# One scan step for two states of one channel block, in a fused AdaLN / Mamba / recurrent kernel

## The chip, the cores and the metric

The kernel runs on one core of one Trainium2 chip. The metric is device time in microseconds (us) of one execution; lower is better. The kernel before took 1357.22 us in the median of three runs (1354.40, 1357.22 and 1361.41).

## What is computed

Two layers run over x of shape (4, 1024, 256). Each layer is adaptive layer norm, a mixer with a gated residual, layer norm, a second part with a gated residual. Layer 0 has dilated attention and a linear layer on block-quantised values. Layer 1 has a Mamba block (a state space scan) and a recurrent gate network. The change is in the scan. Cut to that, the reference is:

```python
xb = silu(causal_conv(x_branch))                    # (B, T, 512 channels)
x_ssm = xb @ x_proj_w                               # B_t, C_t: 16 states each; dt: 1
dt = softplus(dt @ dt_proj_w + dt_proj_b)
A_bar = exp(dt[..., None] * A)                      # (B, T, 512, 16)
Bx = dt[..., None] * B_t[:, :, None, :] * xb[..., None]
def step(h, inp):                                   # over T = 1024, for 512 x 16 states
    a, bx, c = inp
    h = a * h + bx
    return h, jnp.einsum('bds,bs->bd', h, c)
y = (ys + D_param * xb) * silu(z)
out = y @ c_proj_w
```

## The kernel before, in words

The work is cut into G = 8 **halves**: 4 batch rows, each in two halves of TH = 512 time steps. Halves 0, 2, 4, 6 start a batch row, and halves 1, 3, 5, 7 go on from the last states of the half before ("even" and "odd" halves below). The 512 channels are KD = 4 **channel blocks** of 128 partitions. Each block has 16 states, so a half has 64 scans of 512 time steps. They are done in STEPS = 32 **steps** of two scans, 256 steps in all; step m of half g is 32 g + m.

In the kernel before, a step takes one state s of two channel blocks, 2p and 2p+1. These are its operations:

- SyncE fetches row s of B_t and of C_t, broadcast over the 128 partitions (`sp_scan`, 256 KB each, three buffers each).
- ScalarE writes the decay exp(dt A) of each scan into a PSUM bank (`act_decay`, L1200). Scan n uses bank n % 3 and is done in place (`state_bank`, L280). Two of each half's decays, numbers 61 and 62 (`AHEAD`), are computed ahead into SBUF (K[3]) instead, before the softplus of the next half takes ScalarE.
- GpSimd writes dt B_t x for both blocks, 128x1024 (`pool_scan`, L1856), into one of three `inp` buffers once the scans of three steps ago have read it.
- VectorE does the two scans (L1638), copies their last column in even halves (L1646, `carried`), multiplies the states by C_t into one of three `hc` buffers (L1652) and at a block's end multiplies the sum by silu(z) (`dve_gate`, L1611). Where a step's two states lie in banks 2 and 0, copy and product are each done in two instructions (`state_pairs`, L292).
- TensorE adds the two products to two PSUM banks, Y and Y+1, one for each block (`pe_scan`, L846, an identity matmul), which ScalarE has opened with D x (L1227, semaphore dx).

While the scan of half g runs, the same engines do everything else for its neighbours: attention, linear layer, convolution, x_proj and softplus of half g+1 (`*_before`), and c_proj (L780), z (`pe_z`, L677, one PSUM bank, so each waits until VectorE has read the one before, z_ev, L1510), the gate network (L685, L693) and its sums for half g-1 (`*_after`). Each engine's order is written by `in_time` (L127): generators with due times from the table `TIMES`, in quarters of a step, are merged with the engine's scan part. Nothing is reordered later, so an instruction that waits holds all that is queued behind it on its engine.

## Time and profile before

| what | value |
|---|---|
| median of 3 runs | 1357.22 us |
| the profiled execution's own time | 1349.22 us |
| its span, first to last instruction | 1347.9 us |
| VectorE busy | 1243.0 us (92%) |
| TensorE busy | 1156.6 us (86%) |
| GpSimd busy | 984.0 us (73%) |
| ScalarE busy | 808.6 us (60%) |
| DMA traffic | 179.67 MB, 133 GB/s |
| granted TensorE clock, mean | 0.962 |

PE is the matmul part of TensorE and PEld its weight load, DVE is VectorE, ACT ScalarE, POOL GpSimd, SP SyncE. Busy time is the union of an engine's instructions; successive instructions on DVE and ACT overlap in the records by some 80 ns, so the sum of durations is above the busy time. A matmul of float32 shows as two records. "Idle before" is the time in which the engine had nothing running just before the instruction, and the name behind the arrow is what ended it.

### The profile page before, as it was taken

How to read it: one execution, taken by the hardware profiler on the slowest of the kernel's cores; microseconds unless marked ns; L12 is line 12 of the kernel's file. 1: busy time of each engine (PE TensorE's matmuls, PEld its weight loads, DVE VectorE, ACT ScalarE, POOL GpSimd, SP SyncE). 2: the span in 40 equal slices, each digit the busy share in tenths (PEclk: the TensorE clock that was granted, in tenths of full speed). 3: DMA queues.
4: the chain of work that ended last, by engine and by line, in shares of the span. 5: the costliest groups of instructions: out<-in, count | busy, mean ns of one | idle time of the engine just before them, and what ended most of it. 6: DMA issues, size and time to landing. Idle time of an engine off the chain costs nothing.

```text
span 1347.9 us, 12755 instructions
## 1 busy us (share of the span) xinstructions
PE 1156.6 (86%) x3576; PEld 635.3 (47%) x3576; DVE 1243.0 (92%) x1720; ACT 808.6 (60%) x1348; POOL 984.0 (73%) x521
## 2 busy tenths in 40 slices
PE   7667867798999989998999989998999989589984
PEld 5524432473446543574347543564347443333543
DVE  4668999999999999999999999999999999999986
ACT  3247454765777665865776665865776565645432
POOL 3206885689768986899769986899759986885832
PEclk9888988899999999999999999999999999899997
DMA  7304335432534344342534354343533343474611
GB/s 258 117 7 137 109 112 174 115 121 83 181 116 133 112 151 155 127 147 96 177 119 134 109 154 155 123 142 109 167 118 129 110 158 105 131 252 139 220 55 78
DMA packets 92023, 179.67 MB, mean 133 GB/s; under 512 B 10400, under 2 KB 15648, under 8 KB 91696
## 3 DMA queue, kind: packets, MB, share of 16 engines
q1 hardware_dynamic: 88928, 169.55, 39.1%
q10 hardware_dynamic: 3024, 9.31, 1.9%
q8 instruction: 28, 0.46, 0.1%
q14 instruction: 43, 0.35, 0.1%
HBM read 167.51 MB, written 11.31 MB: 133 GB/s over the span
## 4 chain that ended last, share of the span: by engine, by line
DVE 50%; PE 19%; issue 14%; ACT 12%; POOL 4%; DMA 0%; DVEq 0%; SPq 0%; POOLq 0%; ACTq 0%
DVE ps L1638 25%; DVE arena L1652 10%; DVE ps L1346 4%; PE ps L846 4%; PE ps L550 3%; ACT ps L1200 2%; ACT arena L870 2%; POOL arena L1856 2%; DVE stats_before L1239 2%; ACT arena L861 1%; PE ps L596 1%; PE ps L558 1%; PE ps L780 1%; PE ps L677 1%; DVE arena L1611 1%
## 5 line engine op out<-in xcount | busy, mean ns | idle before, releaser
L1856 POOL TENSOR_TENSOR arena<-arena 128x1024 f32<-128x1024 f32 x255 | 598.6, 2363 | 173.1 <-DVE ps L1638 144.6
L1638 DVE TENSOR_TENSOR_SCAN ps<-ps,arena 128x512 f32<-128x512 f32 x498 | 603.6, 1247 | 29.5 <-ACT ps L1200 18.4
L846 PE MATMUL ps<-arena,identF 128*128 128x512 f32 x1024 | 482.0, 603 | 35.8 <-DVE arena L1652 33.6
L1200 ACT ACTIVATE ps<-arena,negA 128x512 f32<-128x512 f32 x498 | 323.8, 683 | 232.0 <-DVE arena L1652 231.0
L1652 DVE TENSOR_TENSOR arena<-ps,arena 128x1024 f32<-128x1024 f32 (+1 forms) x341 | 317.1, 951 | 3.4 <-PE ps L846 0.9
L846 PEld LDWEIGHTS ps<-arena,identF 128*128 128x128 f32 x1024 | 191.5, 194 | 258.5 <-issue 186.3
L861 ACT ACTIVATE arena<-arena,rnln 128x256 f32<-128x256 f32 x128 | 66.2, 589 | 42.8 <-POOL rnln L1668 42.1
L1666 POOL TENSOR_TENSOR rnln<-vnln,consts 128x4 f32<-128x4 f32 x32 | 33.3, 1042 | 74.7 <-DVE vnln L1255 74.7
L596 PE MATMUL ps<-arena,inw 128*128 128x512 f32 x128 | 65.8, 663 | 19.5 <-ACT arena L870 13.3
L677 PE MATMUL ps<-arena,inw 128*128 128x512 f32 x128 | 65.3, 635 | 19.1 <-DVE arena L1510 19.1
L1346 DVE SCALAR_TENSOR_TENSOR ps<-arena,vecs,ps 128x512 f32<-128x512 f32 x96 | 64.7, 749 | 6.6 <-ACT ps L973 6.5
L438 PE MATMUL ps<-identF,arena 128*128 128x128 f32 x248 | 38.6, 299 | 34.5 <-ACT arena L861 17.8
L870 ACT ACTIVATE arena<-ps,modT 128x512 f32<-128x512 f32 x45 | 54.0, 1267 | 16.5 <-PE ps L438 15.8
L780 PE MATMUL ps<-cpw,arena 128*128 128x256 f32 x224 | 57.1, 410 | 6.3 <-DVE arena L1611 6.1
L780 PEld LDWEIGHTS ps<-cpw,arena 128*128 128x128 f32 x224 | 54.6, 327 | 10.6 <-DVE arena L1611 7.3
L438 PEld LDWEIGHTS ps<-identF,arena 128*128 128x128 f32 x248 | 29.9, 153 | 60.8 <-ACT arena L861 18.1
L1677 POOL TENSOR_TENSOR arena<-arena 128x512 f32<-128x512 f32 x42 | 52.9, 1271 | 6.3 <-ACT arena L1042 3.2
L1790 POOL TENSOR_TENSOR arena<-arena 128x1024 f32<-128x1024 f32 x14 | 32.9, 2352 | 33.0 <-ACT arena L1082 33.0
L596 PEld LDWEIGHTS ps<-arena,inw 128*128 128x128 f32 x128 | 25.2, 209 | 58.8 <-issue 26.9
L550 PE MATMUL ps<-arena,wqT 128*128 128x128 f32 (+2 forms) x128 | 40.8, 469 | 10.1 <-ACT arena L870 10.1
L677 PEld LDWEIGHTS ps<-arena,inw 128*128 128x128 f32 x128 | 24.3, 196 | 51.4 <-DVE arena L1510 29.6
L1061 ACT ACTIVATE arena<-ps 128x512 f32<-128x512 f32 x28 | 16.7, 597 | 44.4 <-DVE ps L1346 43.5
(206 smaller groups left out, 1792.6 us busy)
## 6 DMA issues: line engine op xcount, KB each, us to landing
arena<-bc_scratch SPq DMA_DIRECT2D x519, 256.0 KB, 3.5
arena<-in_x SPq DMA_DIRECT2D x16, 256.0 KB, 4.7
arena<-in_x SPq DMA_DIRECT2D x8, 512.0 KB, 6.2
out_x<-arena SPq DMA_DIRECT2D x8, 512.0 KB, 2.7
xr_scratch<-arena SPq DMA_DIRECT2D x6, 512.0 KB, 5.7
px_scratch<-arena SPq DMA_DIRECT2D x6, 512.0 KB, 4.5
arena<-px_scratch ACTq DMA_DIRECT2D x6, 512.0 KB, 4.3
arena<-xr_scratch ACTq DMA_DIRECT2D x6, 512.0 KB, 5.3
```

Source lines behind the costliest of these rows:

```text
L550: x = pe.matmul(ps[:, bank, cols[0]:cols[1]], w[:, h, k, :], hB1[:, k, 0:TH:TH // (cols[1] - cols[0])], start=(k == 0), stop=(k == KE - 1))
L596: x = pe.matmul(ps[:, bank, :], inw[:, k, kd * P:(kd + 1) * P], hB3[:, k, :], start=(k == 0), stop=(k == KE - 1))
L677: x = pe.matmul(ps[:, Y0, :], inw[:, k, DI + kd * P:DI + (kd + 1) * P], hB3[:, k, :], start=(k == 0), stop=(k == KE - 1))
L780: x = pe.matmul(ps[:, Y0, (j % 2) * E:(j % 2 + 1) * E], y2T[:, kd, j:TH:JH], cpw[:, kd, :], start=(kd == 0), stop=(kd == KD - 1))
L846: x = pe.matmul(ps[:, Y + q, :], identF[:], hc[:, m % 3, q, :], start=False, stop=(s == NS - 1), skip_group_check=True)
L861: x = act.activation(dst[:, jj, :], src[:, jj, :], ACT.Identity, bias=rn[:, 1, jj:jj + 1], scale=rn[:, 0, jj:jj + 1])
L870: act.activation(out, src, ACT.Identity, bias=modT[:, layer_col + k, b:b + 1], scale=modT[:, layer_col + 2 + k, b:b + 1]).then_inc(ln[site ...
L1200: act.activation(decay_at(n), dt[:, 2 * p + q, :], ACT.Exp, scale=negA[:, 2 * p + q, s:s + 1]).then_inc(S.decay, 1)
L1346: dve.scalar_tensor_tensor(x, xb[:, kd, tap:tap + TH], vec("conv", kd * TAPS + tap), x, ALU.mult, ALU.add).then_inc(S.conv, 1)
L1638: dve.tensor_tensor_scan(state_bank(n), decay_at(n), inp[:, m % 3, quarter, :], first, ALU.mult, ALU.add).then_inc(S.scan, 1)
L1652: x = dve.tensor_tensor(hc[:, m % 3, q:q + n, :], states, c_at[:, m % 3:m % 3 + 1, :].broadcast_to([P, n, TH]), ALU.mult)
L1856: pool.tensor_tensor(inp[:, m % 3, :, :], u[:, 2 * p:2 * p + 2, :], b_at[:, m % 3:m % 3 + 1, :].broadcast_to([P, 2, TH]), ALU.mult).then_i ...
```

## The change

A step takes two states, 2i and 2i+1, of one channel block kd (`at_step`); a block now has BLOCK_STEPS = 8 steps. What follows:

- The decays of a step fill two neighbouring banks, 0 and 1 or 2 and 3 in turn (`states_of`), always in PSUM; `AHEAD` goes. ScalarE writes those of step m+2 after the product of step m.
- In even halves, from step 1 of the kernel on, one scan instruction of 1024 elements does both states. The decay in the second state's first column must be 0 for that, so the first column of dt is overwritten with a very large number (`dt_cut`) after u is computed, and the decays wait for it. Odd halves and step 0 keep two scans.
- The last column is copied by ScalarE (L1215 of the changed kernel), not by VectorE, and ScalarE waits for its own copy before it overwrites the bank.
- The product is one instruction of 1024 elements, written over `inp` (four buffers in place of three and three of `hc`). GpSimd may write `inp` of step m only when TensorE has added the products of step m-4 (semaphore y); before, it waited for the scans of step m-3.
- One bank of sums, Y = 4. The sum is opened (dx) and gated four times per half, once per block; before, two sums were opened and gated at two places per half. The next block's sum opens when the block before is gated.
- The rows of B_t and C_t are fetched two at a time, 512 KB each.
- xc of the last block has two buffers; c_proj before the last gates takes three blocks, not two; the gate network's "i" shares K[3] with attention; the final stage's buffers move to weights no longer used.
- Every due time of `TIMES` is new.

Two lines of the table of due times, then the core of the rest:

```diff
-        "gate_x": (11, 13, 16.75, 19.75, 22, 24), "gate_c": (11, 14, 16.75, 19.75, 22, 24), "px": (25.25, 26.25),
+        "gate_x": (11.25, 12.5, 17, 17.75, 21, 22.75), "gate_c": (11.25, 12.5, 17, 17.75, 21, 25),
...
-        def state_bank(n):
-
-            return ps[:, n % 3, :]
-
-        def decay_at(n):
-
-
-            if n < 2 * STEPS * (G - 1) and n % (2 * STEPS) in AHEAD:
-                i = AHEAD.index(n % (2 * STEPS))
-                return K[3][:, i * TH:(i + 1) * TH]
-            return state_bank(n)
-
-        def state_pairs(m):
-
-            if m % 3 == 1:
-                return [(0, ps[:, 2:3, :]), (1, ps[:, 0:1, :])]
-            return [(0, ps[:, m % 3 // 2:m % 3 // 2 + 2, :])]
+        def at_step(m):
+
+            return m // STEPS, m % STEPS // BLOCK_STEPS, m % BLOCK_STEPS
+
+        def states_of(m):
+            return ps[:, 2 * (m % 2):2 * (m % 2) + 2, :]
+
+        def together(m):
+
+            return m // STEPS % 2 == 0 and m > 0
+
+        def xc_of(h, kd):
...
             m = step + 2
             if quarter == 0 and 0 <= m < G * STEPS:
...
 
         def sp_program():
...
                 return
-            g, p, s = m // STEPS, m % STEPS // NS, m % NS
+            g, kd, i = at_step(m)
             q = quarter // 2
             if q == 0:
                 pe.wait_ge(S.prod, m + 1)
-            if s == 0:
-                pe.wait_ge(S.dx, 4 * g + 2 * p + q + 1)
-            x = pe.matmul(ps[:, Y + q, :], identF[:], hc[:, m % 3, q, :], start=False, stop=(s == NS - 1),
+                if i == 0:
+                    pe.wait_ge(S.dx, 4 * g + kd + 1)
+            x = pe.matmul(ps[:, Y, :], identF[:], inp[:, m % 4, q, :], start=False, stop=(i == BLOCK_STEPS - 1 and q == 1),
                           skip_group_check=True)
             x.then_inc(S.y, 1)
...
             for b in range(B):
                 act_out(1, b, b)
 
-        def act_decay(n):
-            if not 0 <= n < 2 * G * STEPS:
+        def act_decay(m):
+            if not 0 <= m < G * STEPS:
                 return
-            m, q = n // 2, n % 2
-            g, p, s = m // STEPS, m % STEPS // NS, m % NS
-            if n == 0:
+            g, kd, i = at_step(m)
+            if m == 0:
                 act.wait_ge(S.negA, 2)
                 act.wait_ge(S.modrow, 3)
-            if s == 0:
-                act.wait_ge(S.dt_add, 2 * g + p + 1)
-            act.activation(decay_at(n), dt[:, 2 * p + q, :], ACT.Exp, scale=negA[:, 2 * p + q, s:s + 1]).then_inc(S.decay, 1)
+                act.wait_ge(S.dt_add, 1)
+            elif m == 1:
+                act.wait_ge(S.dt_cut, 1)
+            elif kd % 2 == 0 and i == 0:
+                if g % 2:
+                    act.wait_ge(S.dt_add, 2 * g + kd // 2 + 1)
+                else:
+                    act.wait_ge(S.dt_cut, g + kd // 2 + 1)
+            for q in range(2):
+                x = act.activation(ps[:, 2 * (m % 2) + q, :], dt[:, kd, :], ACT.Exp, scale=negA[:, kd, 2 * i + q:2 * i + q + 1])
+            x.then_inc(S.decay, 1)
 
         def act_scan(step, quarter):
...
                 act.wait_ge(S.prod, m + 1)
-            ahead = 0 <= step < STEPS * (G - 1)
-            for n in (2 * step + 1, 2 * step + 2):
-                if not (ahead and n % (2 * STEPS) in AHEAD):
-                    act_decay(n)
-            if ahead and step % STEPS == AHEAD_STEP:
-
-                act.wait_ge(S.res1, 2 * (step // STEPS + 1) + 2)
-                for n in AHEAD:
-                    act_decay(2 * STEPS * (step // STEPS) + n)
-            if m >= 0 and m % NS == 0:
-
-                g, p = m // STEPS, m % STEPS // NS
-                for q in range(2):
-                    if m:
-                        act.wait_ge(S.gated, 4 * g + 2 * p + q - 1)
-                    else:
-                        act.wait_ge(S.sums_open, 2)
-                        act.wait_ge(S.halved, 1)
-                    act.activation(ps[:, Y + q, :], xc[:, 2 * p + q, :], ACT.Copy, scale=vec("D", 2 * p + q)).then_inc(S.dx, 1)
+                if m // STEPS % 2 == 0:
+
+                    act.activation(carried[:, m % STEPS, :], states_of(m)[:, :, TH - 1], ACT.Copy).then_inc(S.carry, 1)
+                    act.wait_ge(S.carry, STEPS * (m // STEPS // 2) + m % STEPS + 1)
+            act_decay(step + 1)
+            if m >= 0 and m % BLOCK_STEPS == 0:
+
+                g, kd, i = at_step(m)
+                if m:
+                    act.wait_ge(S.gated, 4 * g + kd)
+                else:
+                    act.wait_ge(S.sums_open, 1)
+                    act.wait_ge(S.halved, 1)
+                act.activation(ps[:, Y, :], xc_of(g, kd), ACT.Copy, scale=vec("D", kd)).then_inc(S.dx, 1)
 
         def act_program():
...
 
         def dve_before(h):
             t = before(h)
...
             dve.wait_ge(S.px_mm, 2 * (G - 1) + q + 1)
             dve.tensor_tensor(two(px, q), two_rows(LAST_PX[q]), bias_rows[:, 2:3, :].broadcast_to([P, 2, E]), ALU.add).then_inc(S.px, 1)
 
-        def dve_gate(m, q):
-
-            g, p = m // STEPS, m % STEPS // NS
-            dve.wait_ge(S.z_ev, 4 * g + 4)
-            dve.wait_ge(S.y, 2 * m + 1 + q)
-            dve.tensor_tensor(y2T[:, 2 * p + q, :], ps[:, Y + q, :], sz[:, 2 * p + q, :], ALU.mult).then_inc(S.gated, 1)
+        def dve_gate(m):
+
+            g, kd, i = at_step(m)
+            dve.wait_ge(S.z_ev, 4 * g + kd + 1)
+            dve.wait_ge(S.y, 2 * m + 2)
+            dve.tensor_tensor(y2T[:, kd, :], ps[:, Y, :], sz[:, kd, :], ALU.mult).then_inc(S.gated, 1)
 
         def dve_scan(step, quarter):
             m = step
-            if m == G * STEPS and quarter == 2:
-                for q in range(2):
-                    dve_gate(m - 1, q)
-
-            if quarter == 3 and m % NS == 0 and 0 < m < G * STEPS:
-                dve_gate(m - 1, 0)
-            if quarter == 1 and m % NS == 1 and 1 < m < G * STEPS:
-                dve_gate(m - 2, 1)
+            if quarter == 3 and m % BLOCK_STEPS == 0 and 0 < m < G * STEPS or quarter == 2 and m == G * STEPS:
+                dve_gate(m - 1)
             if not 0 <= m < G * STEPS:
                 return
-            if quarter < 2:
-                n = 2 * m + quarter
-                if quarter == 0:
-                    dve.wait_ge(S.inp, m + 1)
-                dve.wait_ge(S.decay, n + 1)
+            if quarter == 0:
+                dve.wait_ge(S.inp, m + 1)
+                dve.wait_ge(S.decay, m + 1)
+                if together(m):
+                    states = states_of(m).rearrange("p q t -> p (q t)")
+                    dve.tensor_tensor_scan(states, states, inp[:, m % 4, :, :].rearrange("p q t -> p (q t)"), 0.0, ALU.mult,
+                                           ALU.add).then_inc(S.scan, 1)
+                    return
                 if m // STEPS % 2:
-                    first = carried[:, m % STEPS, quarter:quarter + 1]
                     dve.wait_ge(S.carry, STEPS * (m // STEPS // 2) + m % STEPS + 1)
-                else:
-                    first = 0.0
-                if n % (2 * STEPS) in AHEAD and n < 2 * STEPS * (G - 1):
-
-                    dve.wait_ge(S.prod, (n - 3) // 2 + 1)
-                dve.tensor_tensor_scan(state_bank(n), decay_at(n), inp[:, m % 3, quarter, :], first, ALU.mult,
-                                       ALU.add).then_inc(S.scan, 1)
+                for q in range(2):
+                    states = states_of(m)[:, q, :]
+                    first = carried[:, m % STEPS, q:q + 1] if m // STEPS % 2 else 0.0
+                    x = dve.tensor_tensor_scan(states, states, inp[:, m % 4, q, :], first, ALU.mult, ALU.add)
+                x.then_inc(S.scan, 1)
             elif quarter == 2:
-                dve.wait_ge(S.scan, 2 * m + 2)
+                dve.wait_ge(S.scan, m + 1)
                 dve.wait_ge(crow_in[m % 3], 16 * (m // 3 + 1))
-                if m // STEPS % 2 == 0:
-
-                    for q, states in state_pairs(m):
-                        x = dve.tensor_copy(carried[:, m % STEPS, q:q + states.shape[1]], states[:, :, TH - 1])
-                    x.then_inc(S.carry, 1)
-                if m >= 3:
-                    dve.wait_ge(S.y, 2 * m - 4)
-                for q, states in state_pairs(m):
-                    n = states.shape[1]
-                    x = dve.tensor_tensor(hc[:, m % 3, q:q + n, :], states, c_at[:, m % 3:m % 3 + 1, :].broadcast_to([P, n, TH]), ALU.mult)
-                x.then_inc(S.prod, 1)
+                dve.tensor_tensor(inp[:, m % 4, :, :], states_of(m), c_at[:, m % 3, :, :], ALU.mult).then_inc(S.prod, 1)
 
         def dve_program():
...
+                if h % 2 == 0:
+
+                    pool.wait_ge(S.u, 2 * h + p + 1)
+                    pool.memset(dt[:, own, 0:1], LONG).then_inc(S.dt_cut, 1)
 
         def pool_after(g):
...
             m = step + 2
             if quarter or not 1 <= m < G * STEPS:
                 return
-            h, p, s = m // STEPS, m % STEPS // NS, m % NS
+            h, kd, i = at_step(m)
             if m == 1:
                 pool.wait_ge(S.inp, 1)
-            if s == 0:
-                pool.wait_ge(S.u, 2 * h + p + 1)
+            if kd % 2 == 0 and i == 0:
+                pool.wait_ge(S.u, 2 * h + kd // 2 + 1)
             pool.wait_ge(brow_in[m % 3], 16 * (m // 3 + 1))
-            if m >= 3:
-                pool.wait_ge(S.scan, 2 * m - 4)
-            pool.tensor_tensor(inp[:, m % 3, :, :], u[:, 2 * p:2 * p + 2, :], b_at[:, m % 3:m % 3 + 1, :].broadcast_to([P, 2, TH]),
+            if m >= 4:
+                pool.wait_ge(S.y, 2 * m - 6)
+            pool.tensor_tensor(inp[:, m % 4, :, :], u[:, kd:kd + 1, :].broadcast_to([P, 2, TH]), b_at[:, m % 3, :, :],
                                ALU.mult).then_inc(S.inp, 1)
```

**Where instructions move.** VectorE, the start of half 4 (an even half) in the kernel before. Its scans are printed as SCALAR_TENSOR_TENSOR at L1638, the products stand at L1652, the gates of the sums at L1611:

```order
L1638 SCALAR_TENSOR_TENSOR ps<-ps,arena 128x512 [waits decay,inp]
L1638 SCALAR_TENSOR_TENSOR ps<-ps,arena 128x512 [waits decay]
L1646 COPY arena<-ps 128x2 [waits crow_in2,scan]
L1652 TENSOR_TENSOR arena<-ps,arena 128x1024 [waits y]
L1611 TENSOR_TENSOR arena<-ps,arena 128x512 [waits y,z_ev]
L1638 SCALAR_TENSOR_TENSOR ps<-ps,arena 128x512 [waits decay,inp]
L1611 TENSOR_TENSOR arena<-ps,arena 128x512 [waits y,z_ev]
L1638 SCALAR_TENSOR_TENSOR ps<-ps,arena 128x512 [waits decay]
L1338 RECIPROCAL ssum<-ssum 128x4 [waits e_ev]
L1646 COPY arena<-ps 128x2 [waits crow_in0,scan]
L1652 TENSOR_TENSOR arena<-ps,arena 128x1024 [waits y]
L1638 SCALAR_TENSOR_TENSOR ps<-ps,arena 128x512 [waits decay,inp]
L1638 SCALAR_TENSOR_TENSOR ps<-ps,arena 128x512 [waits decay]
```

The same place in the changed kernel (scan L1629, product L1642, gate L1616):

```order
L1629 SCALAR_TENSOR_TENSOR ps<-ps,arena 128x1024 [waits decay,inp]
L1642 TENSOR_TENSOR arena<-ps,arena 128x1024 [waits crow_in2,scan]
L1616 TENSOR_TENSOR arena<-ps,arena 128x512 [waits y,z_ev]
L1629 SCALAR_TENSOR_TENSOR ps<-ps,arena 128x1024 [waits decay,inp]
L1642 TENSOR_TENSOR arena<-ps,arena 128x1024 [waits crow_in0,scan]
L1629 SCALAR_TENSOR_TENSOR ps<-ps,arena 128x1024 [waits decay,inp]
L1642 TENSOR_TENSOR arena<-ps,arena 128x1024 [waits crow_in1,scan]
L1629 SCALAR_TENSOR_TENSOR ps<-ps,arena 128x1024 [waits decay,inp]
L1337 RECIPROCAL ssum<-ssum 128x4 [waits e_ev]
L1332 TENSOR_REDUCE smax<-ps 128x4 [waits s_mm]
L1642 TENSOR_TENSOR arena<-ps,arena 128x1024 [waits crow_in2,scan]
```

The copies are gone, each pair of scans is one instruction, and one gate stands where two stood.

TensorE, half 4 around the sums of step 7, in the kernel before (sums L846, z L677):

```order
L846 MATMUL ps<-arena,identF 128x512 [waits prod]
L846 MATMUL ps<-arena,identF 128x512
L846 MATMUL ps<-arena,identF 128x512 [waits prod]
L677 MATMUL ps<-arena,inw 128x512 [waits z_ev]
L677 MATMUL ps<-arena,inw 128x512
L846 MATMUL ps<-arena,identF 128x512
L846 MATMUL ps<-arena,identF 128x512 [waits prod]
L677 MATMUL ps<-arena,inw 128x512 [waits z_ev]
L677 MATMUL ps<-arena,inw 128x512
L846 MATMUL ps<-arena,identF 128x512
L846 MATMUL ps<-arena,identF 128x512 [waits prod]
```

In the changed kernel (sums L844). The sums of step 7 are now the last of a block, and those of step 8 open the next:

```order
L844 MATMUL ps<-arena,identF 128x512 [waits prod]
L844 MATMUL ps<-arena,identF 128x512
L844 MATMUL ps<-arena,identF 128x512 [waits prod]
L677 MATMUL ps<-arena,inw 128x512 [waits z_ev]
L677 MATMUL ps<-arena,inw 128x512
L844 MATMUL ps<-arena,identF 128x512
L844 MATMUL ps<-arena,identF 128x512 [waits prod]
L844 MATMUL ps<-arena,identF 128x512
L677 MATMUL ps<-arena,inw 128x512 [waits z_ev]
L677 MATMUL ps<-arena,inw 128x512
L844 MATMUL ps<-arena,identF 128x512 [waits dx,prod]
L844 MATMUL ps<-arena,identF 128x512
```

The last z has moved from between the two sums of step 7 to behind them, and the sums of step 8 wait for dx.

## Rows read from the trace of the kernel before

**Rows 1.** The page, busy time, share of the span, instructions.
```profile
PE 1156.6 (86%) x3576; PEld 635.3 (47%) x3576; DVE 1243.0 (92%) x1720; ACT 808.6 (60%) x1348; POOL 984.0 (73%) x521
```
**Rows 2.** Windows, halves 3 and 4: busy of PE, PEld, DVE, ACT, POOL; clock, DMA, GB/s.
```profile
567.97:718.25 150.28, 138.23 (x434) 76.18 (x433) 145.51 (x183) 101.14 (x171) 121.04 (x63) 0.99 0.40 128
718.25:869.75 151.50, 139.88 (x434) 76.78 (x433) 145.68 (x223) 101.24 (x171) 126.86 (x66) 0.98 0.44 140
```
**Rows 3.** Waits of VectorE: for whom, us in total, times, longest.
```profile
DVE ps L1638 <- ACT ps L1200: 18.4, 26, 2.4
DVE ps L1638 <- POOL arena L1856: 10.8, 6, 2.0
```
**Rows 4.** Groups by shape, VectorE: count | busy us, mean ns | idle before.
```profile
L1638 DVE TENSOR_TENSOR_SCAN ps<-ps,arena 128x512 f32<-128x512 f32 x498 | 603.6, 1247 | 29.5 <-ACT ps L1200 18.4 <-POOL arena L1856 10.8
L1652 DVE TENSOR_TENSOR arena<-ps,arena 128x1024 f32<-128x1024 f32 x171 | 208.1, 1217 | 2.6 <-PE ps L846 0.9
L1652 DVE TENSOR_TENSOR arena<-ps,arena 128x512 f32<-128x512 f32 x170 | 108.9, 683 | 0.8
...
L1638 DVE TENSOR_TENSOR_SCAN ps<-arena 128x512 f32<-128x512 f32 x14 | 27.2, 1940 | 0.0
```
**Rows 5.** Order of time, VectorE, two steps of half 0: start us, us.
```profile
174.85 0.22 DVE L1646 COPY arena<-ps 128x1 f32<-128x1 f32 x2
174.99 1.28 DVE L1652 TENSOR_TENSOR arena<-ps,arena 128x512 f32<-128x512 f32 x2
176.19 2.34 DVE L1638 TENSOR_TENSOR_SCAN ps<-ps,arena 128x512 f32<-128x512 f32 x2
178.56 0.16 DVE L1646 COPY arena<-ps 128x2 f32<-128x2 f32 x1
178.64 1.22 DVE L1652 TENSOR_TENSOR arena<-ps,arena 128x1024 f32<-128x1024 f32 x1
```
**Rows 6.** Order of time, VectorE, the end of half 3 and of step 8.
```profile
711.13 2.47 DVE L1638 TENSOR_TENSOR_SCAN ps<-arena 128x512 f32<-128x512 f32 x1
...
718.25 2.35 DVE L1638 TENSOR_TENSOR_SCAN ps<-ps,arena 128x512 f32<-128x512 f32 x2 [1.70 <-POOL arena L1856]
...
755.98 1.27 DVE L1652 TENSOR_TENSOR arena<-ps,arena 128x512 f32<-128x512 f32 x2
```
**Rows 7.** Order of time, GpSimd, the end of half 3.
```profile
712.59 3.18 POOL L1794 TENSOR_TENSOR arena<-arena 128x1024 f32<-128x1024 f32 x1
```
**Rows 8.** Groups by shape, ScalarE.
```profile
L1200 ACT ACTIVATE ps<-arena,negA 128x512 f32<-128x512 f32 x498 | 323.8, 683 | 232.0 <-DVE arena L1652 231.0
...
L952 ACT ACTIVATE arena<-ps,smax 128x128 f32<-128x128 f32 x64 | 22.6, 362 | 6.3 <-DVE smax L1333 6.3
...
L952 ACT ACTIVATION_READ_ACCUMULATOR arena<-ps,smax 128x1 f32 x64 | 12.9, 202 | 0.0
```
**Rows 9.** Order of time, TensorE, half 4: sums, v and c_proj.
```profile
719.75 1.90 PE L846 MATMUL ps<-arena,identF 128*128 128x512 f32 x4
721.49 1.95 PE L558 MATMUL ps<-wvT,arena 128*128 128x128 f32 x16
...
728.44 3.60 PE L846 MATMUL ps<-arena,identF 128*128 128x512 f32 x8
731.87 3.88 PE L780 MATMUL ps<-cpw,arena 128*128 128x256 f32 x16
...
764.02 2.07 PE L846 MATMUL ps<-arena,identF 128*128 128x512 f32 x4
```
**Rows 10.** Groups by shape, GpSimd.
```profile
L1856 POOL TENSOR_TENSOR arena<-arena 128x1024 f32<-128x1024 f32 x255 | 598.6, 2363 | 173.1 <-DVE ps L1638 144.6 <-DVE arena L1453 27.3 <-DMA arena<-bc_scratch 0.5
```
**Rows 11.** DMA issues: KB each, median us to landing.
```profile
arena<-bc_scratch SPq DMA_DIRECT2D x519, 256.0 KB, 3.5
...
px_scratch<-arena SPq DMA_DIRECT2D x6, 512.0 KB, 4.5
```
**Rows 12.** Window with the highest rate, columns as in rows 2.
```profile
15.00:30.00 15.00, 15.00 (x65) 9.48 (x64) 6.57 (x19) 4.35 (x14) 0.24 (x1) 1.00 0.68 276
```

152 lines of the change are left out of this document (79 added, 73 removed), and 32 rows, old and new, of the table TIMES.

## The prediction

> **What bounds the kernel now.** I read the page first. VectorE is busy 92% of the span, more than any other engine [rows 1]. Then the windows of two halves in the middle: VectorE works 145.5 of 150.3 us and 145.7 of 151.5 us, TensorE 138, GpSimd 121 to 127, ScalarE 101 [rows 2]. So in seven of the eight halves the time is VectorE's work plus about 5 us of its waits. TensorE is close behind, and its records have modelled ends, so it has somewhat more room than 138 says. The waits of VectorE come third: the scans wait 18.4 us for decays from ScalarE, in 26 places, and 10.8 us for GpSimd's input [rows 3]. The second of these is one wait per half, at its first step [rows 6]. The groups by shape and the order of time give the price of each VectorE instruction [rows 4, 5]. The forecast is therefore a count of VectorE work removed, corrected by what the new waits can take back.
>
> **The change, part by part.** Durations are from the profiled execution, whose own time is 1349.2 us; the median of the runs is 1357.2 us, 8.0 us more.
>
> *The joint scan.* 127 pairs of scans become one instruction each. A pair takes 2.34 us [rows 5]; a single scan takes 1.25 us in the mean [rows 4], so the two overlap already and little is left to save. No row shows a scan of 1024 elements. The nearest row is the product, which occurs in both forms: two of 512 take 1.28 us, one of 1024 takes 1.22 us [rows 5]. I take that 0.06 us: 127 x 0.06 = 7.6 us gained. At the good end, the fixed part of a product (0.683 us less the 0.534 us that 512 more elements cost [rows 4]) is 0.149 us, which gives 19 us. At the bad end a scan over two banks costs two unoverlapped ones, 2 x 1.247 = 2.49 us, 0.15 us more than the pair: 19 us lost. The Trainium skill (Perfetto Trace Analysis, Optimizing Scalar/DVE Operations) gives a VectorE instruction on PSUM a fixed cost of about 125 ns; by that estimate the joint scans would save 16 us and not 7.6. The rows of pairs speak against counting it in full here, since about half of it overlaps.
>
> *The product.* In 85 of 256 steps it was two instructions and is now one: 85 x 0.06 = 5.1 us [rows 4, 5].
>
> *The copies.* All 171 leave VectorE. Their busy time overlaps their neighbours, so I price them by when the product starts: 0.08 us after a single copy, 0.14 us after a double [rows 5]. 85 x 0.08 + 43 x 0.14 = 12.8 us. On ScalarE each of the 128 copies now costs something between its 202 ns for a column of one element and its 362 ns for 128x128 [rows 8], 26 to 46 us in all, on an engine that works 101 of 150 us per half [rows 2]. I cost that at nothing on the path: the decays of step m+2 are written after the product of step m and are needed only after the scan and the product of step m+1, 2.28 + 1.22 = 3.5 us later, while two decays and a copy take 2 x 0.683 + 0.36 = 1.7 us [rows 8]. If that cover were gone, the copies would cost 26 to 46 us.
>
> *The decays in SBUF.* 14 scans with both inputs in SBUF take 1.94 us against 1.247 us [rows 4]. All decays are in PSUM now: 14 x 0.69 = 9.7 us.
>
> Together 7.6 + 5.1 + 12.8 + 9.7 = 35.2 us of VectorE work.
>
> *Waits for decays, 18.4 us* [rows 3]. Before, the decay of a step's second scan was written after the product before that step, one scan ahead of its use (1.1 us); now it has the 3.5 us above. Some waits stay: where ScalarE does a long block (softplus), and in half 0, where the pipeline fills. I take back 8 us; the bounds are 0 and 18.4.
>
> *The first step of a half, 10.8 us* [rows 3]. The scan waits for GpSimd's chain dt, u, inp. Its u took 3.18 us [rows 7], where products of that size take 2.36 us [rows 10], and a 2.47 us scan from SBUF stands beside it [rows 6]. That scan goes, which gives 0.8 us per half back to the chain; the new overwriting of dt's first column is small and stands in the even halves only. I take 5 us; bounds 0 and 10.8.
>
> *The new waits for sums.* Before, the sums of step 7 were nobody's business: in half 4 they end after 765 us (in the row that begins at 764.02 [rows 9]), while the product of step 8 is done at 757.25 us [rows 6], so TensorE is 8 us late there. Now a gate stands on VectorE right after the product of step 8 and waits for exactly these, and all scans are behind it. The order of TensorE was rewritten for this (the last z has moved behind them). I count what it still has to do between the sums of step 31 of the half before, which end at 721.65 us [rows 9], and those of step 7: 22 matmuls of 512 columns, 24 of 256, 28 of 128. At 0.90, 0.485 and 0.244 us [rows 9] that is 19.8 + 11.6 + 6.8 = 38.2 us at most, since each row ends in a tail. VectorE took from 718.25 to 757.25 us for the same steps, 39.0 us [rows 6], and will take some 2 us less. So TensorE arrives at 3.4 + 38.2 = 41.6 us against 37: up to 4.6 us late, or not at all if it starts earlier and the tails overlap. I take 1.5 us in each of 8 halves, 12 us lost; the bounds are 0 and 8 x 8 = 64 us. The second new wait, of GpSimd's input on the sums of four steps ago, bites at the same point: at 3.6 us per step the input is due 10.8 us after that product and takes 2.36 us [rows 10], so sums up to 8.4 us late cost nothing.
>
> *The rows of B and C.* 512 x 256 KB more is 134 MB, 314 MB in all, 239 GB/s over 1313 us. The kernel has moved 276 GB/s with its queues busy 0.68 [rows 12]. Landing takes 3.5 us for 256 KB and 4.5 us for 512 KB [rows 11], against three steps of 3.6 us from release to use. I cost it at nothing.
>
> **Sum:** 1349.2 - 35.2 - 8 - 5 + 12 = 1313.0 us for the profiled execution, and with the 8.0 us that the median lies above it, **1321 us**.
>
> **Rivals.**
> 1. *TensorE becomes late (slower).* The gates of steps 7 and 23 are new, and TensorE works in order with 138 of 150 us busy [rows 2]. If the sums of step 7 stay 8 us late as they are now, VectorE waits 8 us in each of 8 halves: 1349.2 - 48.2 + 64 = 1365.0, as a median 1373 us. It decides from 6 us per half on (48.2 / 8). For it: the count above leaves no slack. Against it: the order was rewritten just there, and z no longer stands between.
> 2. *The same wait, but 5 to 6 us per half*: it eats the gain, 1349 to 1359 us, no change.
> 3. *The joint scan does not do what it says*: at its bad end it costs 19 us instead of giving 7.6, median 1348 us. For: no row has such a scan. Against: it reads and writes what the pair does.
> 4. *The row fetches bind.* In the shortest steps 1.05 MB in 3.6 us is 291 GB/s, above the 276 shown [rows 12]. At 276 the step is 3.8 us; if half of the 256 steps are that short, 26 us go: median 1347 us. Against: queues busy 0.68 at that rate, and three buffers. By DMA: Bandwidth & Descriptors (Specifications) in the Trainium skill, a core's share of HBM is about 358 GB/s, which would make this rival void.
>
> **How the numbers follow.** A difference of 0.5%, about 7 us, is what a measurement of this kernel can tell from none. The forecast has 0.67; rivals 3 and 4 have 0.05 each and are faster too; rival 2 has 0.11 and rival 1 has 0.12. Faster 0.77, same 0.11, slower 0.12. The low end takes half of what the good bounds add (6 of 11 us for the scan, 5 of 10 for the decays, 3 of 6 at the halves' starts) and about 5 of the 12 us: 1302 us. The high end, 1356 us, takes in rivals 3 and 4 and most of 2, and leaves rival 1 out.
>
> **What would show it.** VectorE busy near 1208 us; no copy of two columns on it; the joint scan at 2.28 to 2.35 us; all scans of 512 at 1.2 to 1.3 us, none at 1.9; waits for decays under 12 us; a new wait of the gate for the sums of about 1 to 2 us per half, after step 8; GpSimd's input waiting for TensorE in place of the scans; DMA near 240 GB/s with landings of the rows under 6 us. A gate that waits over 5 us per half, or ScalarE on the path in even halves but not in odd ones, would prove it wrong.

## The result, and the profile after

| | before | changed |
|---|---|---|
| median (range, runs) | 1356.6 us (1351.3 to 1361.4, 10) | 1348.1 us (1341.8 to 1351.2, 10) |
| profiled execution: own time, span | 1349.2, 1347.9 us | 1350.4, 1349.1 us |
| VectorE busy, idle | 1243.0, 104.9 us | 1219.4, 129.7 us |
| DMA moved | 180 MB | 314 MB |

The ratio is 0.9936, with a 95% interval of 0.9911 to 0.9961; a second measurement of the changed kernel gave 1346.4 us and 0.9933 (0.9908 to 0.9959). The change is faster by 9 us. Forecast were 36.

The page answers to [rows 1], VectorE's groups by shape to [rows 4]. The columns are the same.

```profile
PE 1162.8 (86%) x3574; PEld 639.5 (47%) x3574; DVE 1219.4 (90%) x1338; ACT 818.3 (61%) x1476; POOL 979.5 (73%) x528
```

```profile
L1637 DVE TENSOR_TENSOR_SCAN ps<-ps,arena 128x512 f32<-128x512 f32 x258 | 316.9, 1273 | 12.1 <-ACT ps L1203 8.7 <-ACT arena L1215 2.4 <-POOL arena L1851 1.0
L1642 DVE TENSOR_TENSOR arena<-ps,arena 128x1024 f32<-128x1024 f32 x256 | 312.2, 1219 | 12.6 <-DMA arena<-bc_scratch 6.9 <-issue 0.2
L1629 DVE TENSOR_TENSOR_SCAN ps<-ps,arena 128x1024 f32<-128x1024 f32 x127 | 290.6, 2288 | 19.6 <-ACT ps L1203 17.8 <-POOL arena L1851 1.8
...
L1253 DVE TENSOR_SCALAR vnln<-mvln 128x4 f32<-128x4 f32 x32 | 21.0, 655 | 0.9
```

The parts of the change are all there: joint scans at 2.288 us, every product one instruction at 1.219, no copy on VectorE, no scan at 1.9. Yet busy time fell by 23.6 us where 35.2 were forecast. The last row, which makes -mean after the layernorm moments, is new at this size: an operation on 4 elements takes 0.655 us in the mean, 21.0 us in all; the same 32 took 10.0 us before. These 11 us are nearly all that is missing (23.6 + 11.0 = 34.6), so the count of VectorE's own work was right. The waits of VectorE answer to [rows 3]:

```profile
DVE ps L1629 <- ACT ps L1203: 17.8, 14, 3.7
DVE ps L1637 <- ACT ps L1203: 8.7, 6, 2.1
...
DVE arena L1642 <- DMA arena<-bc_scratch: 6.9, 6, 2.5
```

Waits for decays are 26.5 us instead of 18.4; those for rows of C are new. Five of the decay waits, 10.8 us together, stand at the first scan of halves 2 to 6, where before VectorE waited 8.7 us for GpSimd; all others are 15.7 us. The gate's wait for sums, which the forecast feared, is 2.9 us in all, in two places, both in half 7. The new wait for sums is GpSimd's:

```profile
POOL arena L1851 <- PE ps L844: 142.6, 61, 16.0
```

Most of that is spare time of an engine that isn't the pace (before, it waited 144.6 us for the scans); what it costs is seen below.

Profiles of one kernel start their first scan at different times (before: 110.0 and 115.2 us; the changed kernel: 117.3 and 120.8; its variants: 113.6 to 122.1), so differences of spans below 10 us tell nothing. The lengths of the halves can be compared. I take them from one half's first scan to the next's, the last one to the end of the span:

```
us                 0      1      2      3      4      5      6      7    first scan to end
before           156.5  150.7  150.7  150.3  151.5  150.1  147.9  180.2  1237.9
before_again     158.0  150.7  150.4  150.2  151.0  150.1  148.3  183.3  1241.9
changed          155.2  149.0  146.4  149.0  149.8  149.0  142.3  191.2  1231.8
again_after      155.2  149.0  146.8  149.0  147.1  149.0  143.4  191.5  1231.0
small_ops        155.6  149.0  146.8  149.0  147.9  149.0  142.4  188.3  1228.1
small_pool       155.4  148.6  147.0  148.6  153.1  148.6  142.7  191.5  1235.4
less_z           153.6  147.4  145.3  147.4  145.4  147.4  141.3  188.9  1216.6
less_z_small     154.4  147.5  145.8  148.2  147.0  147.5  142.1  189.6  1222.1
less_z_b         157.8  150.5  149.8  149.7  150.6  149.7  147.3  180.2  1235.7
z_late           158.0  152.7  152.8  153.2  150.8  153.1  146.1  192.6  1259.4
two_scans        155.9  149.0  147.3  149.0  147.7  149.0  143.0  191.3  1232.3
copies_dve       156.2  149.0  146.6  149.0  146.6  149.0  143.0  191.3  1230.8
both_back        155.8  149.0  147.7  149.0  147.7  149.0  143.7  190.1  1232.0
one_row          153.8  149.0  146.4  149.0  146.9  149.0  141.5  186.6  1222.2
k1_late          153.9  147.5  146.1  147.5  146.5  147.5  142.8  189.4  1221.2
loads_spread     155.2  149.0  146.8  149.0  146.9  149.0  142.1  189.3  1227.5
combo            153.8  147.5  147.9  147.5  149.2  147.5  142.8  188.8  1225.0
combo_z          156.6  151.5  150.4  151.3  150.3  151.3  147.1  190.5  1249.0
```

Halves 0 to 6 together gained 18 us (1058 to 1040), and half 7 lost 10 (181.7 to 191.4, means of two). The 9 us are the difference. The odd halves 1, 3 and 5 come out the same to 0.1 us wherever an edit doesn't touch them. The even halves and half 7 don't: 2 to 3 us there can be chance. Part of it has a name. In step 22 of halves 2 and 4 VectorE waits for a load of x, 2.0 us in the first profile of the change, 3.5 us in small_pool, 1.9 us twice in combo; in some profiles of variants it doesn't, and in the three profiles with the old row fetches (before, before_again, less_z_b) and in one_row it never does.

### The profile page after: what moved, and what is told of

Same layout as the page of the kernel before. It is cut to its first block, busy times and chain, and to the rows that moved or that the text cites. A ratio compares the mean times of both kernels' runs of the same rounds, so it can differ in the third digit from the quotient of the medians.

```text
span 1349.1 us, 12381 instructions
## 1 busy us (share of the span) xinstructions
PE 1162.8 (86%) x3574; PEld 639.5 (47%) x3574; DVE 1219.4 (90%) x1338; ACT 818.3 (61%) x1476; POOL 979.5 (73%) x528
## 4 chain that ended last, share of the span: by engine, by line
DVE 39%; PE 22%; issue 13%; ACT 9%; DMA 8%; POOL 8%; SPq 1%; DVEq 0%; POOLq 0%; ACTq 0%
DVE ps L1637 10%; DVE ps L1629 9%; DMA arena<-bc_scratch 7%; DVE arena L1642 6%; PE ps L844 6%; POOL arena L1851 5%; PE ps L550 4%; DVE ps L1345 4%; ACT ps L1203 3%; DVE stats_before L1238 2%; PE ps L590 1%; ACT arena L859 1%; PE ps L596 1%; PE ps L685 1%; DMA arena<-in_x 1%
## 5 line engine op out<-in xcount | busy, mean ns | idle before, releaser
L1851 POOL TENSOR_TENSOR arena<-arena 128x1024 f32<-128x1024 f32 x255 | 597.1, 2360 | 182.2 <-PE ps L844 142.6
L844 PE MATMUL ps<-arena,identF 128*128 128x512 f32 x1024 | 489.2, 610 | 50.1 <-DVE arena L1642 26.9
L1203 ACT ACTIVATE ps<-arena,negA 128x512 f32<-128x512 f32 x512 | 332.6, 683 | 102.6 <-DVE arena L1642 97.5
L1637 DVE TENSOR_TENSOR_SCAN ps<-ps,arena 128x512 f32<-128x512 f32 x258 | 316.9, 1273 | 12.1 <-ACT ps L1203 8.7
L844 PEld LDWEIGHTS ps<-arena,identF 128*128 128x128 f32 x1024 | 190.8, 194 | 283.8 <-issue 218.3
L1642 DVE TENSOR_TENSOR arena<-ps,arena 128x1024 f32<-128x1024 f32 x256 | 312.2, 1219 | 12.6 <-DMA arena<-bc_scratch 6.9
L1629 DVE TENSOR_TENSOR_SCAN ps<-ps,arena 128x1024 f32<-128x1024 f32 x127 | 290.6, 2288 | 19.6 <-ACT ps L1203 17.8
L596 PE MATMUL ps<-arena,inw 128*128 128x512 f32 x128 | 63.9, 647 | 21.3 <-DVE arena L1351 12.1
L439 PE MATMUL ps<-identF,arena 128*128 128x128 f32 x248 | 38.6, 300 | 50.6 <-ACT arena L859 24.8
L677 PE MATMUL ps<-arena,inw 128*128 128x512 f32 x128 | 62.9, 615 | 10.1 <-DVE arena L1515 10.1
L1215 ACT ACTIVATE arena<-ps 128x2 f32<-128x2 f32 x128 | 21.6, 169 | 56.7 <-DVE arena L1642 56.2
L1133 ACT ACTIVATE arena<-ps,vecs 128x512 f32<-128x512 f32 x48 | 32.3, 673 | 37.9 <-PE ps L693 29.3
L677 PEld LDWEIGHTS ps<-arena,inw 128*128 128x128 f32 x128 | 24.2, 195 | 41.1 <-issue 23.5
```

Source lines behind the costliest of these rows:

```text
L439: x = pe.transpose(ps[:, bank, j * P:(j + 1) * P], src[:, j, k * P:(k + 1) * P], identF[:])
L596: x = pe.matmul(ps[:, bank, :], inw[:, k, kd * P:(kd + 1) * P], hB3[:, k, :], start=(k == 0), stop=(k == KE - 1))
L677: x = pe.matmul(ps[:, Y0, :], inw[:, k, DI + kd * P:DI + (kd + 1) * P], hB3[:, k, :], start=(k == 0), stop=(k == KE - 1))
L844: x = pe.matmul(ps[:, Y, :], identF[:], inp[:, m % 4, q, :], start=False, stop=(i == BLOCK_STEPS - 1 and q == 1), skip_group_check=True)
L1203: x = act.activation(ps[:, 2 * (m % 2) + q, :], dt[:, kd, :], ACT.Exp, scale=negA[:, kd, 2 * i + q:2 * i + q + 1])
L1629: dve.tensor_tensor_scan(states, states, inp[:, m % 4, :, :].rearrange("p q t -> p (q t)"), 0.0, ALU.mult, ALU.add).then_inc(S.scan, 1)
```

## The experiments

Times are medians; the kernel before ran beside each at 1356.3 to 1357.5 us. All edits are to the changed kernel unless said otherwise.

**Second profiles.** The two kernels as they are.

> The changed kernel as it is, a second profile and its times. The profile of before lies 7.3 us under its own median and that of the change 2.3 us over its own, so two profiles can't tell which differences belong to the change. What both theories below need is fixed: if the 11 us on the 4-element operations (21.0 us in 32 instructions against 10.0 us before), the last half (191.2 us against 180.2) and the first scan (117.3 us against 110.0) belong to the order of instructions, each comes back within 2 us; what does not come back was chance of one execution. Time: 1348 us, ratio to before 0.991 to 0.996.

> The kernel before as it is, for a second profile. Three profiles of the change and its variants start their first scan at 114.5 to 120.8 us, the only profile of before at 110.0. If the start is chance of the execution (its loads), before's first scan comes later this time, at 113 to 119 us, and the stretch from the first scan to the end stays at 1237.9 us within 2 us (1231.8 and 1230.9 us in the change). If the order of the change makes the start late, it comes back at 110 us.

Measured: the changed kernel at 1346.4 us, its 4-element group at 21.0 us again and half 7 at 191.5; before at one time of 1358.4 us, half 7 at 183.3. The 4-element group and the longer half 7 come back with the changed kernel; half 7 of before grew by 3.1 us, and its stretch behind the start by 4.0, where I had expected 2 at most. The start doesn't come back, or by little: it moved by 5 us in before and by 3.5 in the change, and with the variants (113.2 us for the one of before, from 113.6 for those of the change) the two ranges overlap. That the medians differ by 9 us and the stretches behind the start by 8.5 (means of two) says the same.

**The 4-element operations.** First in another form, then on GpSimd. One line of two is shown each time; var + eps is moved alike.

```diff
-dve.tensor_scalar(vn[:, 1, :], mv[:, :, 0], -1.0, None, ALU.mult)
+dve.scalar_tensor_tensor(vn[:, 1, :], mv[:, :, 0], -2.0, mv[:, :, 0], ALU.mult, ALU.add)
```

> Only the 32 operations of 4 elements that follow the layernorm moments are written in another form: scalar_tensor_tensor with the same source twice (-2m+m and max(v+eps, v), the same values) in place of tensor_scalar. Theory 1, small operations: a tensor_scalar from SBUF to SBUF can't start or end while a GpSimd instruction runs beside it, and the new order puts them beside GpSimd's 2.36 us products; then the group falls from 21.0 us to 10 or less, VectorE's work from 1219 to about 1208 us, and the time by up to 11 us (1337 to 1343 us). Theory 2, the doubled row fetches take the gain: the group may fall, but the time stays at 1348 us within 3 us, since rows of B and C come when they come. If the new form is locked out as well, the group stays at 21 us and nothing is told of the time.

Measured: 1349.4 us, ratio 0.9945 (0.9924 to 0.9966); the group stays at 20.8 us. This was the third case of the expectation, which tells nothing of the time.

```diff
-dve.tensor_scalar(vn[:, 1, :], mv[:, :, 0], -1.0, None, ALU.mult)
+pool.tensor_scalar(vn[:, 1, :], mv[:, :, 0], -1.0, None, ALU.mult)
```

> The 32 operations of 4 elements after the layernorm moments leave VectorE: GpSimd makes -mean and var + eps itself, just before the power that it takes of them. Written as scalar_tensor_tensor they were held as long (20.8 us), so the form was not what held them. Theory 1, small operations: they are held while a GpSimd product runs beside them, and they stand on the path, since VectorE is; then all of their 21.0 us leave VectorE's work (1219 to 1198 us), odd halves shorten from 149.0 to about 147 us, even ones by 2 to 3 us, and the time falls by 10 to 17 us, to 1331 to 1338 us. Theory 3, other waits are next in line (decays, GpSimd's products, TensorE): busy time falls as much, but idle time rises by more than half of it, and the time falls by less than 6 us.

Measured: 1351.8 us, ratio 0.9979 (0.9959 to 0.9999). VectorE's busy time fell by 15.5 us, to 1203.9, and by the medians the kernel became 4 to 5 us slower, not faster; an odd half gained 0.4 us. In the profile half 4 stands out with 153.1 us, 3.5 of them the wait for x. VectorE's waits name what was behind:

```profile
DVE arena L1512 <- ACT arena L1098: 12.0, 10, 1.8
```

That is the product with the tanh of z (4.0 us of waits in the changed kernel), and the tanh waits for TensorE's z:

```profile
ACT arena L1098 <- PE ps L677: 27.0, 16, 3.5
```

Theory 1 falls in its second half: the operations were held, but taking them off VectorE gave nothing. This alone doesn't say which engine paced it, since GpSimd got their work (busy 994.9 us, 979.5 before the edit). The windows of half 3, steps 0 to 3, 4 to 7 and 8 to 11, point at TensorE. Before:

```profile
568.00:584.30 16.30, 16.30 (x76) 13.34 (x75) 16.23 (x18) 10.69 (x28) 15.72 (x7) 1.00 0.57 188
584.30:601.50 17.20, 17.20 (x73) 12.47 (x72) 17.17 (x28) 9.91 (x20) 16.61 (x10) 1.00 0.39 136
601.50:622.20 20.70, 18.18 (x44) 7.70 (x43) 19.45 (x31) 13.04 (x21) 18.55 (x12) 0.92 0.30 100
```

Changed:

```profile
567.90:583.50 15.60, 14.74 (x66) 11.00 (x66) 15.50 (x15) 9.22 (x20) 15.52 (x8) 1.00 0.83 300
583.50:604.80 21.30, 21.30 (x84) 14.98 (x84) 21.13 (x37) 12.92 (x30) 18.10 (x12) 1.00 0.66 248
604.80:622.40 17.60, 12.53 (x34) 4.87 (x33) 17.50 (x20) 11.07 (x17) 16.13 (x9) 1.00 0.70 236
```

And small_pool, steps 4 to 7:

```profile
586.50:607.10 20.60, 20.60 (x82) 14.62 (x82) 19.01 (x32) 12.89 (x30) 17.95 (x14) 1.00 0.73 257
```

The first busy column is TensorE, the third VectorE. In the change TensorE has no gap in steps 4 to 7 and 5 us of room in steps 8 to 11; with 2.1 us of VectorE's work gone, the stretch is 0.7 us shorter and VectorE idle for the rest. A full engine is no proof, though: TensorE was full in steps 0 to 7 before the change, too. And the new due times put more of VectorE's own work there as well, 37 records in steps 4 to 7 for 28. In order of time, in the changed kernel, TensorE, GpSimd and VectorE at that place:

```profile
591.63 1.02 PE L844 MATMUL ps<-arena,identF 128*128 128x512 f32 x2
592.49 1.05 PE L572 MATMUL ps<-arena 128*128 128x128 f32 x8
593.38 1.88 PE L844 MATMUL ps<-arena,identF 128*128 128x512 f32 x4
```

```profile
592.80 2.37 POOL L1851 TENSOR_TENSOR arena<-arena 128x1024 f32<-128x1024 f32 x1 [1.86 <-PE ps L844]
595.41 2.37 POOL L1851 TENSOR_TENSOR arena<-arena 128x1024 f32<-128x1024 f32 x1 [0.24 <-PE ps L844]
```

```profile
596.55 1.25 DVE L1253 TENSOR_SCALAR vnln<-mvln 128x4 f32<-128x4 f32 x1
597.72 0.16 DVE L1254 TENSOR_SCALAR vnln<-mvln 128x4 f32<-128x4 f32 x1
597.79 2.45 DVE L1637 TENSOR_TENSOR_SCAN ps<-ps,arena 128x512 f32<-128x512 f32 x2
```

GpSimd's input waited for TensorE's sums (the new wait), so its product ran late, until 597.78 us; VectorE's operation on 4 elements ends at 597.80. The scan behind it had its input since 595.17 and its decays since 597.08 at the latest, so it was held for nothing else. What the profile counts as VectorE's work is a wait for GpSimd's product, and by it for TensorE at second hand.

**Less work for TensorE.** In pe_z one matmul in place of two:

```diff
-for k in range(KE):
-    x = pe.matmul(ps[:, Y0, :], inw[:, k, ...], hB3[:, k, :], start=(k == 0), stop=(k == KE - 1))
+x = pe.matmul(ps[:, Y0, :], inw[:, 0, ...], hB3[:, 0, :], start=True, stop=True)
```

> The z projection takes one of its two blocks of the contraction (its second half is left out, so the output is another): TensorE does 0.94 us less for each of four z's, 3.8 us less per half, at steps 4 to 10; all else as in the change. Theory 4: the first steps of a half are TensorE's. In steps 4 to 7 of half 3 it is busy 21.3 of 21.3 us, and VectorE too, 21.1, but with 4-element operations that are held by GpSimd; TensorE at work without a gap is what the z's wait for, and taking VectorE's work off alone gave nothing (small_pool: 149.0 to 148.6 us). Then here each engine still stands in for the other, and an odd half shortens by under 1 us, the time by 0 to 6 us. If TensorE alone bound these steps, an odd half would shorten by 2 to 3 us (146.5 us) and the time by 14 to 20 us. Theory 3b, TensorE has room: 149.0 us as it was.

Measured: 1333.6 us, ratio 0.9833 (0.9807 to 0.9859), 13 to 15 us less than the change. My expectation, two engines that stand in for each other (0 to 6 us), was wrong, and the branch "TensorE alone" is the near one, with 1.6 us per odd half against its 2 to 3 and 13 to 15 us against its 14 to 20. TensorE's busy time fell by 20 us, VectorE's instructions are the same, and the 4-element group shrank with TensorE, from 21.0 to 11.6 us. Steps 4 to 7 of half 3, and the instruction that took 1.25 us above:

```profile
575.50:595.10 19.60, 19.60 (x80) 13.99 (x80) 19.43 (x36) 13.58 (x32) 18.00 (x12) 1.00 0.76 270
```

```profile
588.52 0.38 DVE L1251 TENSOR_SCALAR vnln<-mvln 128x4 f32<-128x4 f32 x1
588.82 0.16 DVE L1252 TENSOR_SCALAR vnln<-mvln 128x4 f32<-128x4 f32 x1
```

The edit also makes each z arrive sooner. That is the lesser part: the waits for the tanh fell from 4.0 to 2.2 us.

> Both edits at once: the z projection at half its work on TensorE (its second half left out) and the 4-element operations on GpSimd. Theory 4, two engines full in the same steps: either edit alone gives under 1 us per half, both together 1.5 to 2.5 us per half, so odd halves at 146.5 to 147.5 us and the time 10 to 18 us under the 1347 to 1348 us of the change, though small_pool alone stood at 1351.8. If neither was on the path (decays or GpSimd's products are), both together give what they gave alone, under 1 us per half, and the time stays over 1345 us.

Measured: 1340.8 us, ratio 0.9880 (0.9858 to 0.9903), 7 us slower than less_z alone, and an odd half no shorter. Theory 4 asked for under 1 us per half from either edit alone; less_z alone gave 1.6, so it falls. That the operations cost more on GpSimd than on VectorE is shown by the medians twice (4 to 5 us, 7 us); why, only argued: there they stand ahead of its products. By the same token neither run shows what VectorE would gain if these operations cost nothing anywhere.

The same halving of z in the kernel before:

> The kernel before with the z projection at half its work on TensorE (its second half left out, so the output is another). In the change the same edit gave 1.6 us per odd half and 14.6 us from the first scan to the end. Theory 5, TensorE became the pace by the change, since VectorE's work fell and the gates and GpSimd's input now wait for sums: here the edit gives under 0.5 us per half (150.3 us stays over 149.8) and 0 to 4 us in all. Theory 6, TensorE was the pace of the first steps already (busy 33.5 of 33.5 us in steps 0 to 7 of half 3): the edit gives 1 to 2 us per half and 8 to 15 us in all.

Measured: 1350.6 us, ratio 0.9963 (0.9943 to 0.9984), 5 to 6 us less than the kernel before; 0.2 to 0.8 us in each of halves 1 to 6 (against the mean of the two profiles of before), 4 us from the first scan to the end against a gain of 15 in the change. This lies between the two theories and nearer to theory 5: TensorE, though full in steps 0 to 7, was near the pace before and became the pace by the change.

```diff
-"pe_after": {... "z": (4.25, 6, 7.5, 8.75)
+"pe_after": {... "z": (4.25, 7.75, 8.75, 9.5)
-"act_after": {... "z_tanh": (6, 7.75, 7.75, 9.25)
+"act_after": {... "z_tanh": (6, 8.75, 9.25, 10)
-"dve_after": {... "z": (6.75, 7.75, 8.25, 10.25)
+"dve_after": {... "z": (6.75, 9.25, 9.75, 10.5)
```

> The change with nothing left out, but TensorE's second, third and fourth z put later: due at steps 7.75, 8.75 and 9.5 in place of 6, 7.5 and 8.75, their tanh and product moved with them. In steps 4 to 7 of half 3 TensorE is busy 21.3 of 21.3 us, in steps 8 to 11 12.5 of 17.5 us. If TensorE's work in steps 4 to 7 is the pace, one or two z's of 1.88 us leave it and fit into the room behind: those steps shorten from 21.3 to about 19.5 us, an odd half to 147 to 148 us, and the time by 7 to 14 us. If the z's only move their wait along (VectorE waits for the tanh in steps 8 to 10), steps 8 to 11 grow by what steps 4 to 7 lose and the time stays within 3 us of 1347.

Measured: 1378.9 us, ratio 1.0179 (1.0148 to 1.0209), 31 us slower, which neither branch foresaw: the wait moved along and grew. Steps 4 to 7 of half 3 shortened from 21.3 to 20.5 us, steps 8 to 11 grew from 17.5 to 22.5.

```profile
DVE arena L1515 <- ACT arena L1098: 32.8, 17, 3.4
```

All four z's pass through one bank, from TensorE to ScalarE to VectorE and back; three in a row, 1 step apart, make VectorE wait for each. The clock adds to it. In half 3 TensorE stands idle for 5.6 us until VectorE has read the bank, and the z behind that gap (four records) takes twice as long as the one before it:

```profile
612.32 1.88 PE L677 MATMUL ps<-arena,inw 128*128 128x512 f32 x4
...
621.56 3.78 PE L677 MATMUL ps<-arena,inw 128*128 128x512 f32 x4 [5.64 <-DVE arena L1515]
```

TensorE's granted clock is 1.00 (2.4 GHz) in steps 4 to 7 and 0.50, its lower level (1.2 GHz), from 621.5 to 625.4 us. So this run prices idle time and a low clock as well as the place of the z's. Whether another placement of TensorE's work pays is open; this one doesn't.

**The joint scan and the copies.**

```diff
-                if together(m):
+                if False:
```

> The changed kernel with the joint scan taken apart again: in even halves two scans of 512 elements, all else as in the change. The profile has 127 joint scans at 2.288 us where a pair took 2.34 us; by the forecast's count 127 x 0.05 to 0.06 us = 6.5 to 7.6 us go, so 1354 to 1356 us, with VectorE's busy time up by 127 x (2 x 1.25 - 2.29) = 27 us, of which most overlaps. If VectorE is covered by waits for other engines in even halves (theory 2, or ScalarE late), less than 3 us go. A gain would mean that the long scan holds something else up, such as the start of the decays.

Measured: 1349.0 us, ratio 0.9952 (0.9931 to 0.9973). Even halves 2 and 6 are within 1 us of the change, half 0 is 0.7 longer: 0 to 3 us in all, at most 0.02 us per scan, not 0.06.

```diff
-act.activation(carried[:, m % STEPS, :], states_of(m)[:, :, TH - 1], ACT.Copy).then_inc(S.carry, 1)
-act.wait_ge(S.carry, STEPS * (m // STEPS // 2) + m % STEPS + 1)
+act.wait_ge(S.decay, m + 2)
+dve.tensor_copy(carried[:, m % STEPS, :], states_of(m)[:, :, TH - 1]).then_inc(S.carry, 1)
```

> The 128 copies of the last column go back from ScalarE to VectorE, between scan and product, as one instruction of two columns each; all else as in the change. By the forecast's prices (the product starts 0.08 us later after a single copy, 0.14 us after a double one) 10 to 18 us come back in even halves, less 2.4 us of waits for ScalarE's copies at the carried states: 1355 to 1363 us. If ScalarE's 21.6 us of copies cost decays as much as they give VectorE, the time stays at 1347 us within 3 us. Odd halves stay at 149.0 us or gain 0.2.

Measured: 1347.0 us, ratio 0.9944 (0.9923 to 0.9964), as the change. The copies add 6.9 us to VectorE's busy time (1226.3), and the waits for decays fall by 7.8 us (26.6 in the second profile of the change):

```profile
DVE ps L1627 <- ACT ps L1203: 13.5, 9, 3.0
...
DVE ps L1635 <- ACT ps L1203: 5.3, 4, 2.6
```

On ScalarE a copy stands ahead of two decays; what it saves VectorE it takes back there. This was the expectation's second branch.

> Two parts of the change taken back at once: in even halves two scans of 512 in place of one of 1024, and the copies of the last columns on VectorE. Alone each gave next to nothing (even halves 0.7 us longer with two scans, the same with the copies on VectorE), where 1.9 and 3.2 us were forecast. If they stand in for each other, since even halves have another floor (TensorE and the decays) just under them, even halves grow by 2 to 3.5 us to about 149 to 150 us and the time to 1355 us or more. If each really is worth what it gave alone, they grow by 0.7 to 1 us and the time stays at 1347 to 1351 us.

Measured: 1353.2 us, ratio 0.9970 (0.9953 to 0.9987), by the medians 5 to 7 us slower than the change; in the profile even halves grew by about 1 us and the stretch from first scan to end by 0.6. Both parts together are worth 1 to 7 us, where 20.4 were forecast; medians and profile don't pin it down further.

**The rows of B and C.** One row fetched per step for both states, for B as for C:

```diff
-sp.dma_start(c_at[:, m % 3, :, :], bc_d[h:h + 1, NS + 2 * i:NS + 2 * i + 2, :].broadcast_to([P, 2, TH]))
+sp.dma_start(c_at[:, m % 3, 0, :], bc_d[h, NS + 2 * i:NS + 2 * i + 1, :].broadcast_to([P, TH]))
```

> A step fetches one row of B and one of C (256 KB each, as before the change) and both of its states use them, so half of the row traffic is gone and the second state of each step is computed with the first one's rows (the output is another). Instructions of all engines are the same in number and shape. Theory 2, the doubled fetches cost what is missing: DMA falls from 314 to 180 MB, the 6.9 us of VectorE's waits for C rows go, the last half goes from 191 us back to about 182, and the time falls by 10 to 20 us, to 1328 to 1338 us. Theory 1, small operations and waits for ScalarE: only the waits for C rows go, and the time falls by 3 to 7 us, to 1341 to 1345 us; under 3 us means that the fetches cost nothing.

Measured: 1343.5 us, ratio 0.9897 (0.9862 to 0.9931), by the medians 3 to 5 us less, which is theory 1's range (the two intervals overlap); from the first scan to the end 9 us less, 5 of them in half 7, where theory 2 had 9. VectorE's waits for rows of C are gone, 5.8 and 6.9 us in the two profiles of the change. In half 7 the loads of the final stage come on top, in the changed kernel's window (DMA share and GB/s last):

```profile
1180.00:1190.00 10.00, 3.10 (x7) 1.10 (x6) 7.49 (x16) 2.78 (x5) 5.14 (x3) 0.84 1.02 412
```

The rate alone isn't the limit that rival 4 took it for: steps 0 to 3 of half 3 moved 300 GB/s with no such wait, and these 412 GB/s lie above both its 276 and its 358.

```diff
-yield t + (19.25 if hf else 4.25) + b * 2
+yield t + (19.25 + b * 2 if hf else 3.25 + b * 5)
```

> Only the six 512 KB loads for the final stage in the last half are spread: one each 2.5 steps from step 3.25 to 15.75, in place of one a step from 4.25 to 9.25. In the change the rows of C arrive late in steps 5 and 6 of that half (1.0 and 2.4 us) with the DMA engines busy 0.95 to 1.0, and half 7 takes 191.2 and 191.5 us (180.2 and 183.3 before). If the loads collide with the doubled row fetches, half 7 shortens by 3 to 5 us to 186.5 to 188.5 us and the time by as much. If the rows are late for their own bulk, the waits spread to later steps and half 7 stays at 190 to 192 us.

Measured: 1344.7 us, ratio 0.9916 (0.9890 to 0.9943); half 7 at 189.3 us, 2.1 less; VectorE's waits for C rows there fell from 5.1 to 1.9 us. That is less than the 3 to 5 us expected, and it isn't clear of chance: small_ops and k1_late leave these loads where they were and have half 7 at 188.3 and 189.4 us, with 1.4 and 2.2 us of such waits. The collision stands in the trace; what spreading the loads is worth is open.

**ScalarE at a half's first step.**

```diff
-"k1": 4, "v0": 9.25
+"k1": 4.5, "v0": 9.25
```

> Only ScalarE's order changes, at one place per half: the decays of a half's first step now stand ahead of its evacuation of k1, which waits 1.8 to 2.5 us for TensorE. In the change the first scan of halves 2 to 7 waits 2.1 to 2.2 us for these decays, and GpSimd's input for it ends at 719.2 us where the scan starts at 720.7 (half 4), 570.6 against 571.7 (half 3). If ScalarE's order took the place of GpSimd as what the half's start waits for, each of six halves shortens by 1.1 to 1.5 us, the wait turns into one for GpSimd of 0.7 to 1 us, and the time falls by 7 to 9 us, to 1338 to 1341 us. If later waits in the half (decays at step 27, sums) take it back, odd halves stay at 149.0 us.

Measured: 1343.2 us, ratio 0.9919 (0.9895 to 0.9944), by the medians 3 to 5 us less than the change (7 to 9 expected; the two intervals overlap). The profile is clearer: odd halves went from 149.0 to 147.5 us, even ones by 0 to 1.4, and the stretch from first scan to end by 10 us, 2 of them in half 7 and perhaps chance. ScalarE, first in the changed kernel (second profile), then in k1_late, and below the scan that waits, the same two:

```profile
718.85 0.60 ACT L1006 ACTIVATE arena<-ps 128x512 f32<-128x512 f32 x1 [2.53 <-PE ps L550]
719.35 1.30 ACT L1203 ACTIVATE ps<-arena,negA 128x512 f32<-128x512 f32 x2
```

```profile
714.71 1.30 ACT L1203 ACTIVATE ps<-arena,negA 128x512 f32<-128x512 f32 x2 [0.59 <-POOL arena L1789]
716.65 0.60 ACT L1006 ACTIVATE arena<-ps 128x512 f32<-128x512 f32 x1 [0.64 <-PE ps L550]
```

```profile
720.74 2.30 DVE L1629 TENSOR_TENSOR_SCAN ps<-ps,arena 128x1024 f32<-128x1024 f32 x1 [2.20 <-ACT ps L1203]
```

```profile
717.05 2.30 DVE L1629 TENSOR_TENSOR_SCAN ps<-ps,arena 128x1024 f32<-128x1024 f32 x1 [0.70 <-POOL arena L1851]
```

The decays wait behind an evacuation that waits for TensorE: again TensorE, at second hand.

> The change with two edits that each gave something alone: ScalarE's decays ahead of k1 (1221.2 us from the first scan to the end against 1231.4) and the loads of the final stage spread (1227.5). If the two add, 1217 us, the time 13 to 14 us under the change's 1347: 1333 to 1336 us.

Measured: 1341.3 us, ratio 0.9896 (0.9865 to 0.9927). That misses the 1333 to 1336 expected, and the stretch of 1225.0 us misses 1217; 3.8 of these 8 us are the two waits for x. It is the fastest whole version by its median of six, but no measurable step beyond k1_late.

> combo with the later z's as well. If all three losses are separate, 1205 to 1212 us from the first scan to the end and 1322 to 1329 us in all, near the 1321 that was forecast for the change. If z_late gives nothing alone, as combo: 1333 to 1336 us.

Measured: 1373.6 us, ratio 1.0130 (1.0100 to 1.0159), outside both branches: the later z's cost 32 us here as they cost 31 alone.

## Why the prediction was wrong in size

Direction and range held (1348 in 1302 to 1356), the size didn't: 9 us of 36.

- **VectorE's work as the pace: the step that failed.** "In seven of the eight halves the time is VectorE's work plus about 5 us of its waits" was read from sums per half [rows 2]. It holds over a half and not within it: in steps 0 to 7 TensorE was busy without a gap before, too. The change took work off VectorE and stacked TensorE's at steps 4 to 7 (21.3 us, 84 matmul records, where 17.2 us and 73 stood before). Halving z, 20 us off TensorE, gave 13 to 15 us in the change and 4 to 6 before it; taking 15.5 us off VectorE and onto GpSimd gave none.
- **TensorE's lateness: the term of 12 us.** The count of "38.2 us at most" up to the sums of step 7 was good: halves 2 to 6 show the same 22, 24 and 28 float32 matmuls (of 512, 256 and 128 columns) and 38.6 to 39.1 us. What failed is where the lateness comes out. I priced it as a wait of the gate, and that waits for nothing in halves 0 to 6, because in halves 2 to 6 VectorE reaches it 40.5 to 41.0 us after the half's first scan and not 37. I also wrote that sums up to 8.4 us late cost nothing on GpSimd's input. The scans hardly waited for that input (2.8 us in all), but the product shifted, and VectorE's 4-element operations were held until its end; behind them stood a scan whose input was ready. Beside these two forms there are the decays behind k1. Rival 1 named the mechanism and looked for it at the gate alone. z and k1 show 13 to 15 and 3 to 10 us of it; the full price wasn't measured.
- **Joint scan, 7.6 us:** its duration was right (2.288 of 2.28), its worth 0 to 3 us.
- **Copies, 12.8 us:** worth 0 alone. "Nothing on the path" for ScalarE was wrong: without its copies the waits for decays are 7.8 us shorter.
- **Product and SBUF scans, 14.8 us:** never undone alone, so argued only. Odd halves, where neither joint scan nor copy is, gained 1.4 us, and these two terms make 2.0 (0.65 + 1.39) of their forecast; but the terms for waits fall there as well, so the 1.4 can't be given to them. The 1.94 us of a scan from SBUF is also no price of one thing. Of the 14, six had no GpSimd instruction beside them and took 1.21 to 1.27 us; eight had, and took 2.38 to 2.73:

```profile
708.68 1.27 DVE L1638 TENSOR_TENSOR_SCAN ps<-arena 128x512 f32<-128x512 f32 x1
710.16 2.35 POOL L1790 TENSOR_TENSOR arena<-arena 128x1024 f32<-128x1024 f32 x1 [5.64 <-ACT arena L1082]
711.13 2.47 DVE L1638 TENSOR_TENSOR_SCAN ps<-arena 128x512 f32<-128x512 f32 x1
```

  The 9.7 us were time held by GpSimd, the same thing that then grew at the 4-element operations by 11.
- **The first step of a half, 5 us to be gained, and the decays, 8 us.** The wait for GpSimd fell from 10.8 to 2.8 us, but ScalarE took its place. The waits before the first scans of halves 1 to 7 grew from 10.8 to 14.2 us in all: 2.1 to 2.2 us in halves 2 to 6 for decays held up behind k1. These are also why waits for decays grew to 26.5; elsewhere they fell from 18.4 to 15.7, under 3 of the 8 us.
- **DMA at nothing:** wrong by 3 to 9 us, about half of it in half 7, where other loads come on top, and some in the waits for x; the rate in the mean (233 GB/s) told nothing of that.
- **Half 7, about 10 us lost,** wasn't looked at by itself. With single rows it was 5 us shorter, with halved z 2.5; but edits that touch neither shortened it by 2 to 3, so the split is open.

## What to carry to other kernels

An engine with 92% busy need not pace a kernel in every stage: cut windows as fine as the schedule's stages before pricing work removed from it. A full engine in such a window is a suspect and no more; take work off it there and see, in the kernel before as well as after. An in-order engine's lateness shows up at second hand, as another engine's wait or even as a long "busy" operation; in this trace a 4-element instruction that took 1.25 us was a wait. Work given to an engine with room is free only if nothing that the path needs is queued behind it.

## What the runs showed of the hardware

VectorE's operation on 4 elements in SBUF takes 0.17 us alone and up to 2.09 us when a GpSimd product runs beside it, and ends with that product (597.80 against 597.78 us). A one-source and a two-source form were held alike (21.0 and 20.8 us), and so were scans with both inputs in SBUF (1.21 to 1.27 us alone, 2.38 to 2.73 us beside GpSimd's work), while products that read PSUM and SBUF beside the same GpSimd instructions took at most 1.23 us. The Trainium skill (SBUF — State Buffer, SBUF: two separate sides) has this as an exclusive lock that VectorE takes in a two-port mode or with two SBUF inputs, and that GpSimd holds for a whole instruction; the traces agree with both cases. One scan over 1024 elements in two banks takes 2.288 us, a pair of 512 took 2.34. After a TensorE gap of 5.6 us a z took 3.78 us at a granted clock of 0.50, where it took 1.88 us at 1.00.
